# Constant matmuls between TensorE's own work, and batch 0's side work dealt anew over its steps

## What is computed

```python
xn = layernorm(x)
# Mamba, 256 inner channels i, 16 states s
xz = rmsnorm(xn) @ in_proj_w.T ;  x_s, z = split(xz)
u = silu(causal_conv4(x_s) + conv_b)
dt_raw, B, C = split(u @ x_proj_w.T)            # 8, 16, 16
delta = softplus(dt_raw @ dt_proj_w.T + dt_proj_b)
h_t = exp(delta_t * A) * h_(t-1) + delta_t * u_t * B_t
y = sum_s(h * C) + u * D_param
attn = (y * silu(z)) @ out_proj_w.T + xn
# experts
top2 of xn @ w_router.T, softmax of the two
ffn = sum over the two of gate * (silu(xn @ w_gate[e]) * (xn @ w_up[e])) @ w_down[e]
out = x + attn + ffn
```

## Time and profile before

| what | value |
|---|---|
| time, median of 3 runs | 666.46 us (665.41 to 667.42) |
| the profiled execution | 663.5 us, its span 661.7 us |
| DVE busy | 607.0 us (92%) |
| PE busy | 548.3 us (83%) |
| POOL busy | 502.1 us (76%) |
| ACT busy | 420.8 us (64%) |
| mean granted TensorE clock | 0.920 of full |

### The profile page before, as it was taken

The page is one execution under the profiler, slowest core; times in us unless marked ns, Lnnn a source line. Parts: engine busy times, 40 slices in busy tenths (PEclk is TensorE's granted clock), DMA queues, the critical chain, the costliest instruction groups (busy, mean ns, idle before and its releaser), DMA issues.

```text
span 661.7 us, 11259 instructions
## 1 busy us (share of the span) xinstructions
PE 548.3 (83%) x3474; PEld 431.8 (65%) x3474; DVE 607.0 (92%) x867; ACT 420.8 (64%) x839; POOL 502.1 (76%) x504
## 2 busy tenths in 40 slices
PE   5987687789799988999789987999876885768687
PEld 2456465647778777787678777877764653646564
DVE  6969959999999998999999999999999878789977
ACT  1886786047656765557755676558664588569691
POOL 5795059359898798968988798987968868658771
PEclk9889978778899997999989999999999667889979
DMA  7550401425776885879758787768843343223531
GB/s 226 160 174 5 190 1 63 136 85 179 262 253 224 278 271 192 287 230 315 251 190 297 222 292 271 261 231 296 250 179 140 151 163 144 79 80 108 150 100 42
DMA packets 59197, 122.88 MB, mean 186 GB/s; under 512 B 8314, under 2 KB 39426, under 8 KB 52098
## 3 DMA queue, kind: packets, MB, share of 16 engines
q1 hardware_dynamic: 53922, 112.39, 49.1%
q0 software_dynamic: 4496, 9.45, 5.5%
q10 hardware_dynamic: 720, 0.33, 0.2%
HBM read 112.70 MB, written 9.44 MB: 185 GB/s over the span
## 4 chain that ended last, share of the span: by engine, by line
PE 43%; DVE 22%; issue 13%; ACT 13%; POOL 6%; DMA 2%; DVEq 0%; ACTq 0%
DVE bank L1064 9%; PE bank L1468 7%; PE bank L1342 7%; PE bank L1374 6%; DVE h_sb L1081 5%; PE bank L1482 5%; PE bank L1476 4%; POOL dbu L877 3%; PE bank L1305 2%; ACT dbu L512 2%; ACT da L484 2%; PE bank L1397 2%; PE bank L1443 2%; PE bank L1389 2%; PE bank L1354 2%
## 5 line engine op out<-in xcount | busy, mean ns | idle before, releaser
L877 POOL TENSOR_TENSOR dbu<-du,xn_all 128x512 f32<-128x512 f32 x178 | 223.3, 1277 | 64.9 <-DVE bank L1064 64.6
L1064 DVE TENSOR_TENSOR_SCAN bank<-bank,dbu 128x512 f32<-128x512 f32 x176 | 214.3, 1221 | 3.9 <-ACT bank L496 3.9
L496 ACT ACTIVATE bank<-delta,a_sb 128x512 f32<-128x512 f32 x176 | 121.7, 692 | 98.0 <-DVE h_sb L1081 96.4
L1081 DVE TENSOR_TENSOR h_sb<-bank,xh_all 128x512 f32<-128x512 f32 x240 | 158.9, 676 | 1.2
L1342 PE MATMUL bank<-id_sb,h_sb 128*128 128x128 f32 x992 | 143.1, 292 | 15.7 <-DVE h_sb L1081 12.7
L1342 PEld LDWEIGHTS bank<-id_sb,h_sb 128*128 128x128 f32 x992 | 123.0, 152 | 27.3 <-DVE h_sb L1081 20.9
L1064 DVE TENSOR_TENSOR_SCAN bank<-da,bank 128x512 f32<-128x512 f32 x76 | 89.9, 1215 | 24.4 <-PE bank L1305 23.0
L1468 PEld LDWEIGHTS bank<-wd_sb,hid 117*128 117x128 f32 (+1 forms) x432 | 56.4, 194 | 63.1 <-issue 37.4
L1468 PE MATMUL bank<-wd_sb,hid 117*128 117x128 f32 (+1 forms) x432 | 65.9, 289 | 32.7 <-ACT xT L655 22.1
L1305 PE MATMUL bank<-id_sb,dbu 128*128 128x128 f32 x304 | 55.0, 314 | 36.7 <-ACT dbu L512 25.5
L864 POOL DMA_INDIRECT xs<-xn_rows,src x72 | 70.7, 982 | 11.1 <-issue 5.7
(11 more groups left out here) (186 smaller groups left out, 833.0 us busy)
## 6 DMA issues: line engine op xcount, KB each, us to landing
xh_all<-b_rows SPq DMA_DIRECT2D x30, 1024.0 KB, 7.2
xn_all<-b_rows SPq DMA_DIRECT2D x25, 1024.0 KB, 7.5
wgu_sb<-in_w_gu SPq DMA_DIRECT2D x72, 352.0 KB, 4.1
wd_sb<-in_w_dn SPq DMA_DIRECT2D x72, 192.0 KB, 5.3
y_slots<-ys SPq DMA_DIRECT2D x72, 64.0 KB
xn_rows<-xn_all SPq DMA_DIRECT2D x8, 256.0 KB, 3.3
out<-x_sb SPq DMA_DIRECT2D x7, 256.0 KB, 7.0
x_sb<-in_x SPq DMA_DIRECT2D x2, 640.0 KB, 6.0
```

The lines of the kernel that those rows point to most:

```text
L496: nc.scalar.activation(bank_of(b, m)[:, :], delta[b % 2][:, hf, :], ACT.Exp, scale=a_sb[:, hf, k:k + 1]).then_inc(s["da_rdy"], 1)
L877: nc.gpsimd.tensor_tensor(dbu[k % 2][:, hf, :], du[b % 2][:, hf, :], b_ring[c % 2][:, k % CH, :], ALU.mult).then_inc(s["dbu_p"], 1)
L1064: nc.vector.tensor_tensor_scan(at, da_of(n)[:, hf, :] if n in IN_SBUF else at, inp, 0.0, ALU.mult, ALU.add).then_inc(s["h_rdy"], 1)
L1081: nc.vector.tensor_tensor(h_sb[k % 2][:, hf, :], bank_of(b, 2 * k + hf)[:, :], row, ALU.mult).then_inc(s["p_rdy"], 1)
```

## The change

Five things change. PE gets a new helper `keep`, a matmul of the identity and the convolution's weights into bank columns that nobody reads. It stands once in each of steps 0 to 5 of batch 0 (240 columns), twice in steps 12 to 15 (384 columns each), once in steps 0 to 3 of batch 1 (512), in steps 12 to 15 of batch 5 and in every step of batches 6 and 7 (256 columns where the next step is in `BY_PE`, else 512; in all 9 of 512 and 23 of 256 in batches 6 and 7). `skip(b)` for b from 1 to 5 moves from step 15 to step 8, behind the rest of that step. Batch 0's own two halves of `skip` move from steps 10 and 11 to 7 and 8. The convolution of batch 1's second half is cut in two over steps 2 and 3 (it stood whole in step 1), that of batch 2's first half over steps 9 and 10 (whole in step 9), and its second half moves to steps 12 and 13. And the rest of batch 0's side work is dealt anew: logits, late rows, half_tanh and unit, steps_mm, totals and ranking, the logarithm, the gate weights and the z gate, which gets a bank of its own (`z_bank`).

```diff
-    TURNED, SKIPPED, SKIPPED0 = 11, (1, 2), (10, 11)
+    TURNED, SKIPPED, SKIPPED0 = 11, (1, 2), (7, 8)
+        z_bank = lambda b: FB[0] if b else UB
-        LATE_ROWS = {2: (24, 28), 4: (28, 32)}
+        LOGITS_AT = {0: (1, 2), 1: (3,), 2: (4,), 3: (5,), 5: (6,), 6: (7,)}
+        LATE_ROWS = {0: (24, 28), 4: (28, 32)}
-            return {14: 1, 15: 0} if b == 0 else {8: 1, 10: 0} if b == 6 else {4: 1, 6: 0}
+            return {13: 1, 15: 0} if b == 0 else {8: 1, 10: 0} if b == 6 else {4: 1, 6: 0}
...
             def step0(k):
 
-                if k == 0:
-                    half_tanh(1, 0)
                 if 0 < k < S - 1:
                     scaled(k + 1)
+                if k in z_step(0):
+                    z_gate(0, k)
                 if k + 2 < S:
                     decay(k + 2)
...
-                if k == 2:
-                    half_tanh(1, 1)
-                if k == 4:
+                if k in (0, 4):
+                    half_tanh(1, k // 4)
+                if k == 6:
                     rows(1)
                 if k in (7, 8):
                     magnitudes(1, k - 7)
                     vanishing(1, k - 7)
-                routing(k)
                 if k == 8:
                     rounded(1)
                     corrected(1)
+                    totals_out()
+                    logarithm(1)
+                    ranks_out()
                 if k == 9:
-                    logarithm(1)
-                if k in (10, 13):
-                    half_tanh(2, k // 13)
-                if k in z_step(0):
-                    z_gate(0, k)
+                    spread_choices()
+                if k in (11, 14):
+                    half_tanh(2, k // 14)
...
             act.wait_ge(s["a_ready"], 2)
             decay(0)
-            xh_out(3)
+            decay(1)
             input_turned(0)
             scaled(1)
-            decay(1)
+            xh_out(3)
...
-                if k in (0, 2):
-                    unit(1, k // 2)
+                if k in (1, 4):
+                    unit(1, k // 4)
                 if k == 7:
                     choices()
-                if k in (10, 13):
-                    unit(2, k // 13)
-                if k == 11:
-                    weights()
+                if k in (11, 14):
+                    unit(2, k // 14)
                 if k in z_step(0):
                     z_gate(0, k)
+                if k == 15:
+                    weights()
...
+            def keep(at, start=True):
+
+                MM(at, id_sb[:, :], wk_flat[:, 0:at.shape[1]], start=start, stop=True, skip_group_check=True)
...
-                if k == 1:
-                    conv(1, 1, range(K))
-                if k == 3:
+                if k in (2, 3):
+                    conv(1, 1, (2 * k - 4, 2 * k - 3))
+                if k == 5:
                     rows(1)
+                if k in SKIPPED0:
+                    skip(0, (SKIPPED0.index(k),))
                 if k == 8:
                     totals()
-                if k == 9:
                     ranking()
-                    conv(2, 0, range(K))
-                if k in (11, 12):
-                    conv(2, 1, (2 * k - 22, 2 * k - 21))
+                if k in (9, 10):
+                    conv(2, 0, (2 * k - 18, 2 * k - 17))
+                if k in (12, 13):
+                    conv(2, 1, (2 * k - 24, 2 * k - 23))
...
-                if k in (6, 7):
-                    steps_mm(1, k - 6)
+                if k == 7:
+                    steps_mm(1, 0)
+                    steps_mm(1, 1)
+                if k < 6:
+                    keep(LGB[:, 2 * C - 2 * H + 2 * E:])
+                if k >= 12:
+                    keep(MAP[:, P:], k == 12)
+                    keep(MAP[:, P:], False)
...
-                if k == S - 1 and 0 < b < NB - 2:
-                    skip(b)
...
+                if 0 < b < NB - 2 and k == LOG_AT[b]:
+                    skip(b)
+                if b == 1 and k < 4:
+                    keep(UB[:, :])
+                if b > 5 or b == 5 and k >= 12:
+                    i = sum(m < g for m in SUM_AT)
+                    if i < NB:
+                        wait(pe, "ga_rdy", NJ)
+                        wait(pe, "comb", i - 1)
+                        keep((GB, UB)[i % 2][:, 0:256 if g + 1 in BY_PE else 512])
...
+            conv(1, 0, range(K))
+            columns(0)
             logits(0)
-            logits(1)
-            columns(0)
-            conv(1, 0, range(K))
             xh_turn(3)
             input_turn(0, 0)
-            logits(2)
```

34 lines of the change are left out of this document (16 added, 18 removed).

## The result

The changed kernel took **660.07 us** (median of 4 runs, 659.36 to 662.08) against 666.94 us for the kernel before on the same chip (4 runs, 665.41 to 667.78). The ratio is 0.9904, with an interval from 0.9875 to 0.9933: 6.4 us or 1% faster (the two medians lie 6.9 us apart). The forecast was 654, with a range from 649 to 659, so half of the 12.5 us came and the time lies outside the range.

What follows compares the result with a forecast made beforehand. DVE was taken as busy for most of the span, with idle time in batches 0, 6 and 7. Batch 0 (7.0), batches 1 to 5 (3.5) and 6 and 7 (2.0) sum to 12.5 us: median 654, range 649 to 659.

Steps and rivals of the forecast that it cites:

- late rows (2.4): Batch 0: late rows moved to step 0 cost some 1.1 us and stand in a wait there; 2.4 us saved.
- gate weights (2.6): Batch 0: gate weights moved to step 15 take 1.7 us in place of 4.3; 2.6 us saved.
- Waits of batch 0 (3.0): Batch 0: DVE's waits for PE and ACT fall from 14.6 to 11.6 us; 3.0 us saved.
- 1.0 off for the low clock in batch 0: Batch 0: 1.0 us taken off the 8.0 us sum for a low clock somewhere in the crowded steps, leaving 7.0.
- Batches 1 to 5 (3.5, up to 4.6): Batches 1 to 5: skip moved into PE's idle time at step 8 saves 3.5 us, between 0 and 4.6.
- Batches 6 and 7 (+2.0): Batches 6 and 7: the keeps bring 2.0 us net (5 - 1 - 2), between -6 and 6.
- The 1.0 for the last sum: End of batch 7: the keep before the last gathered sum is paid whole, 0.94, put at 1.0 us lost.
- The 5 us that a held clock was to bring: Batches 6 and 7: half of the low-clock waits at gathered sums go, winning 5 us.
- Rival 1: Keeps don't hold the clock, each run before the long wait; batches 6 and 7 give -2 or so: 658; chance 0.15.
- Rival 2: PE becomes the bound of batch 0; waits 16 in place of 11.6, 7.0 becomes about 2.6: 658; chance 0.15.
- Rival 3: Matmuls hold the clock everywhere, where turns alone would not; batches 6 and 7 give 7: 649; chance 0.10.
- Rival 4: Slower: the keeps, 19.3 us, lie on the path of batches 6 and 7: 675; chance 0.05.

Runs made afterwards that it cites:

- first pair: The changed kernel and the kernel before, measured together on one chip: 660.07 us against 666.94, ratio 0.9904.
- series 2: Runs on one chip of the kernel before (663.85 us), the changed kernel (ratio 0.9918), both unchanged, and dve_moves (0.9862).
- dve_moves: before_skip8 with the late rows at step 0 instead of 2 and the weights at step 15 instead of 11: 657.78 us against 663.85, ratio 0.9862.
- pe_deal: The changed kernel without keeps, with late rows back at step 2 and weights back at step 11: ratio 0.9849 against the kernel before.
- before_again: The kernel before, unchanged, run again for a second trace: ratio 0.9990.
- before_skip8: The kernel before with one edit, skip of batches 1 to 5 at step 8: 664.13 us against 672.13, ratio 0.9883.
- series 4: Runs on one chip: the kernel before 672.69 us, the changed kernel 667.12, keeps_67 665.97, no_keeps_2 658.72.
- keeps_67: The changed kernel with the keeps of batches 6 and 7 alone: 665.97 us against 672.69 for the kernel before, ratio 0.9910.
- no_keeps_2: The changed kernel without any keep, run once more: 658.72 us against 672.69 for the kernel before, ratio 0.9812.
- after_again: The changed kernel, unchanged, run again: ratio 0.9918 against the kernel before.
- keeps_67_small: keeps_67 with every keep at 64 columns in place of 256 or 512: ratio 0.9896 against the kernel before.
- series 1: Runs on one chip that include the kernel before (672.13 us) and before_skip8 (664.13 us, ratio 0.9883).

## Why the prediction was right or wrong

The forecast missed in these steps: the late rows (2.4) and the gate weights (2.6), which it counted as gains and which brought nothing; the waits of batch 0, which it put at 11.6 us with the keeps in place and which were 15.8; and batches 6 and 7, where it put +2.0 for the keeps and they cost. Batches 1 to 5 gave 3.2 more than forecast and hid a part of that, so that half of the 12.5 us came is in part luck.

Seen over all traces, the sum comes out so. The changed kernel starts batch 1 at 137.08, 133.75 and 136.70 us, the kernel before at 136.35 and 138.28: 1.5 us on the average. Batches 1 to 5 give 6.3 and 7.0, 6.7. Batches 6 and 7 on the chips of the first pair and of series 2 take 153.5 and 154.0 against 149.3 and 150.6: 3.8 lost. In all 4.4, beside 6.4, 5.4 and 4.5 by the three ratios of the pair (0.9904, 0.9918, 0.9933).

- **Late rows (2.4) and weights (2.6): failed.** These two terms are the largest part of what didn't come in batch 0. I took what a DVE instruction is lengthened by for a cost of its place. It is a cost of meeting POOL (weights), paid by the next instruction if it isn't paid by this one, or a cost of meeting POOL inside a stretch that others set (late rows). dve_moves measures the pair at nothing, and pe_deal the same beside PE's new order; 0.3 us is left of the weights. The weights themselves came out at 1.07 us in dve_moves and 2.0 in the changed kernel, near the 1.7 forecast; what I left out was who stands in the stretch after them.
- **Waits of batch 0 (3.0): failed with the keeps, about right in size without them.** In the profiled execution DVE waited 15.8 us for turns where 11.6 were forecast: 4.69 and 0.92 at step 1 for 2.4, 1.72 at step 2 for 0.4, 4.1 at steps 3 and 4 for 4.0, 4.1 at steps 9 to 11 for 4.8, and 0.26 elsewhere. Without keeps PE's order brings 3.3 us. Steps 9 and 10 won 3.5 where the forecast had 2.3 for steps 8 to 11. Step 1's second half waited too long since all that stood ahead of it ran at 1.2 GHz, the logits above all (3.42 us for 1.92).
- **1.0 off for the low clock in batch 0:** in the profiled execution the low clock met steps 1 and 2 (0.50 and 0.59 on the average) and hardly steps 12 to 15 (0.92), and it is the start's keeps that cost, 3.3 us in steps 0 to 8 by the averages, with 0.9 back at steps 9 and 10.
- **Batches 1 to 5 (3.5, up to 4.6): the mechanism right, the size too small.** I took 3.5 of 4.6 us of waits and all of them went: DVE's idle time fell from 8.7 to 4.1. The bound was too low as well, since DVE's busy time fell with it, from 367.3 to 365.6, with the same instructions. Two that follow each other without a wait overlap a little in the record (two scans of 1.23 us take 2.33, two products of 0.67 take 1.27), and one that waits loses that. Half of the waits went, 13 of 26. The durations of DVE's 500 instructions sum to the same in before_again and before_skip8 (407.2 us), and what overlaps of them is 39.7 us in the one and 41.5 in the other, 1.7 more; I hadn't counted it.
- **Batches 6 and 7 (+2.0): the sign failed.** The 1.0 for the last sum is 0.85. The 5 us that a held clock was to bring didn't come, although the clock of batch 6 rose as forecast (0.88 in all three traces of the changed kernel, above the 0.85 named). The low stretches were fewer, but met sums all the same, and the keeps, put at 2.0 for all places but the last, cost more: without them the same kernel is 7.3 us faster (series 4). DVE waited 22.5 us for turns in keeps_67 for 18.0 in no_keeps_2.
- **The rivals.** Rival 1 (the keeps don't pay in 6 and 7; 658) is nearest in kind. Rival 2's waits of 16 us in batch 0 stood at 15.8 in the profiled execution and at 12.9 in after_again, where batch 0 took 98.3 us. Rival 3 is out: turns alone had run at 1.00, and they bring the full clock back by themselves. In no_keeps_2 PE executed only turns and accumulate's transposes from 522.70 on, at a granted clock of 0.50 until 525.70, and from 525.80 it was 1.00. And no_keeps_2 has a lower ratio than any kernel with keeps. Rival 4's cost is real at a third of the keeps' 19.3 us (6.6), below the 55% from which it would have eaten the gain; that it is time of their own on the path is shown at two places only, and keeps_67_small speaks against it as the main part.
- **Two readings of the prediction.** The stretch from 512.36 to 593.60, called batch 6, holds the first step of batch 7 as well; batch 6 itself took 76.3 us, at a clock of 0.73. And the range left out the low ends of its own stages: even two of them, 662.5 us, lie beyond its 659, and the measured 660.07 fell between.

The kernel that beats both is the changed one without keeps: 0.9812 on one chip with 0.9933 for the changed kernel, and 0.9834 beside 0.9883 for the moved skip alone, there with intervals that overlap.

## What to carry to other kernels

When an instruction is slow only beside another engine's work, look what would stand in that stretch if it were moved, before its excess is counted as a gain. Matmuls put in to hold the clock have to be judged by whether the dense, awaited steps run faster, not by the mean clock; here they raised the mean and cost 8 us. Real work moved into an idle stretch (the skip) gave 6.3 to 7.0 us and added none; constants in that same stretch were not tried. And a wait removed is worth a little more than the view lists, because the two instructions around it overlap again.

## What the runs showed of the hardware

- Batch 6 of one and the same kernel took 77.6 and 73.5 us in two executions, with a clock of 0.72 and 0.84, while its batches 1 to 5 repeated to 0.1 us. The spans of the unchanged kernel before on one chip (before_again, 12 executions) lie between 657.2 and 665.8 us.
- The last batch is 4 to 10 us longer in some series than in others, with the code of before in it too. The windows from its first scan to the end are 73.00 us in before (588.70 to 661.70), and in before_skip8:

```profile
580.94:661.40 80.46, 60.24 (x326) 43.66 (x324) 64.28 (x79) 52.44 (x115) 45.56 (x58) 0.89 0.33 97
```

  The traces of series 1, 3, 4 and 5 have 79.5 to 84.2 there, those of series 2 and the first pair 73.0 to 76.4. The longer ones have it in steps 4 and 8 of batch 7 (5.0 to 7.3 and 6.9 to 8.6 us, where the others have 4.0 and 4.0 to 4.2), two steps with a gathered sum. The chip's number alone doesn't settle it: series 1 and 2 are both recorded on chip 4, with medians of 672.13 and 663.85 us for the kernel before. Why, no run here shows; it is the reason why the last columns of the table compare within a series alone.
- A one-hot of 128x1024 that meets POOL's products waited for more than one of them: 1.76 us longer, a product being 1.29. By its end, 0.54 us behind the pair's, the second product went ahead of it as well. The late rows ended 0.85 us behind POOL's products, whether they had begun at 53.11 (before) or at 52.04 (before_again).
- The full clock came back while PE ran nothing but fp32 transposes (no_keeps_2, 522.70 to 525.80, 0.50 to 1.00).
